# Attention before a soft mixture of experts: order of the first loads, place of the sums of values, and GpSimd keeping the statistics

## The chip, the cores and the metric

One Trainium2 chip, of which the kernel uses 1 core. The metric is the device time of one execution in microseconds (us). Names used: PE is TensorE, ACT is ScalarE, DVE is VectorE, POOL is GpSimd, SP is the engine that issues the transfers.

## What is computed

The input x has 8 batches of 512 tokens with 256 features. Only the attention half matters here:

```
xn   = layernorm(x)                                   # per token, no scale or shift
q,k,v = xn @ w_qkv.T, split into 16 heads of 16
dots = q @ k.T                                        # per head, no softmax
attn = dots / max(norm(dots over j), 1e-12) * g + b   # g, b: one number per head
out  = (attn @ v) @ w_out.T + b_out
x    = x + layernorm(out)
```

A second block follows, a soft mixture of 8 experts with 128 slots each (dispatch and combine weights by softmax, two weight layers with GELU, layernorm, residual). The change does not touch it.

## The kernel before

**Method.** As the attention has no softmax, the 512 x 512 scores are never formed. With G = xn^T xn (256 x 256, the "Gram" product), k^T v = wk G wv^T, so per batch the kernel computes G, then G times the key weights (`gk`), then per pair of head groups the head products k^T k and k^T v (`heads`), masked to the diagonal blocks of the heads. The outputs are q times the masked k^T v, the squared norms are sums over q * (k^T k q) (`qGq`). The bias b of the attention multiplies the sum of the values over the tokens, `vb`, which comes from the sums of xn over the tokens (`xsum`, an extra column of the Gram product) times the value weights: `value_sums`. Queries do not come from xn: they use the raw x transposed in DRAM (`xT`), with weights whose column mean has been subtracted, as the missing division by the standard deviation cancels in the normalised scores.

**Precision.** TensorE multiplies float32r operands. Each float32 operand is split in a rounded high part (ACT writes it, `round_...`) and the rest (DVE subtracts, `rest_of_...`), and a product takes three passes: high x high, high x low, low x high. So ahead of each product stands the chain ACT rounding, DVE rest. From batch 3 on the Gram product takes two passes and is completed by its own transpose (`transpose_gram`, `add_transposed`).

**Order.** Each engine has one hand-written instruction stream, and semaphores tie them together. Attention is a software pipeline over batches: in step b, PE's `attention(b)` runs the front of batch b and the back of batch b - 1 in this order: `gram_of_x(b)` (L821), `gram_times_q(b-1)` (L894), `transpose_gram(b)` (L830), `outputs(b-1)` (L904), `norms(b-1)` (L914), `queries(b)` part 0 (L884), `gram_times_k(b)` (L843), `queries(b)` part 1 (L884), in batches 0, 1, 3, 5 and 7 `value_sums(b)` (L865), `transpose_o(b-1)` (L922), `head_products(b)` (L854), `projection(b-1)` (L931). Batches 3 to 6 are a hardware loop of two steps; "odd" in the code is the odd batch, which computes the sums of two batches at once in bank 0 of PSUM. Norms and Gram times keys share bank 3. Batch 0 has a front only.

ACT's `attention(b)` copies the Gram, takes squares and roots of the layer norms of batch b - 2 (L1407, L1414, L1427), keeps the sums of x (`keep_xsum`, L1350), rounds the Gram (L1364), copies the queries (`keep_qT`, L1381), rounds `gk` (L1374) and the transposed outputs `oT` (L1395), and then xn and xT of the next batch (L1314, L1316, L1332). DVE's `attention(b)` adds the projection's bias (L2126), takes the statistics of batch b + 1 (L1990, L1995), `qGq` (L2082), the Gram's rest (L2046), clamps the norms (L2090), inverts and scales the outputs (L2097, L2101), normalises batch b + 1 (`norm_x`, L2008, four tiles), copies its mean and variance to `mv_x` and its floor to `norm_floor` (L2014, L1938), in odd batches `vb` (`keep_sums`, L2071), then the rest of `gk` (L2076), the rest of `oT` (L2112), the masked heads (`keep_heads`, L2061 and L2062), and the rest of the next xn and xT (L2030, L2034).

**Opening.** SP issues, in this order: x of batch 0 in two halves, the identity, query weights, key and value weights, xT of batch 0 (L555 to L560), and after x has landed the next loads. DVE's `norm_first` normalises batch 0 in halves and then copies its statistics. PE sums the query weights (L965), DVE centres them (L1932). Then, before batch 0's products, ACT rounds key and value weights (L1452), query weights (L1454) and xT (L1332), and DVE takes the rests in the same order (L1926, L2034), then the Gram's (L2049). PE's `queries` wait for both weight parts, `gram_times_k` for the first.

POOL has in the attention stage only the centring of the output weights and bias (L707, L710); later it works on the dispatch weights.

## Time and profile before

| | |
|---|---|
| median of 3 runs | 821.07 us (820.95 to 821.4) |
| the profiled execution | 820.74 us, its span 818.9 us |
| busy share of the span | PE 99%, weight loads 88%, DVE 85%, ACT 77%, POOL 21% |
| granted TensorE clock | full in all 40 slices of the span |
| attention stage | from the start to about 149 us, where the projection beside batch 7's front ends |

A page of the profile describes one execution. Busy shares are averages over stages; for the question what a reordering is worth, the chain of waits (what released each instruction, followed back from the end) and the timelines of the engines in the attention stage are the views to read. Matmuls overlap in their pipeline, so their listed durations are longer than the distance from one to the next.

### The profile page before, as it was taken

How to read it: one execution, taken by the hardware profiler on the slowest of the kernel's cores; microseconds unless marked ns; L12 is line 12 of the kernel's file. 1: busy time of each engine (PE TensorE's matmuls, PEld its weight loads, DVE VectorE, ACT ScalarE, POOL GpSimd, SP SyncE). 2: the span in 40 equal slices, each digit the busy share in tenths (PEclk: the TensorE clock that was granted, in tenths of full speed). 3: DMA queues.
4: the chain of work that ended last, by engine and by line, in shares of the span. 5: the costliest groups of instructions: out<-in, count | busy, mean ns of one | idle time of the engine just before them, and what ended most of it. 6: DMA issues, size and time to landing. Idle time of an engine off the chain costs nothing.

```text
span 818.9 us, 16585 instructions
## 1 busy us (share of the span) xinstructions
PE 807.9 (99%) x5186; PEld 718.8 (88%) x5186; DVE 699.0 (85%) x1373; ACT 630.4 (77%) x1269; POOL 168.4 (21%) x211
## 2 busy tenths in 40 slices
PE   8999999999999999999999999999999999999997
PEld 7888888888888888887998999999999999999997
DVE  8798988799999989998958888888888889487776
ACT  5676766667786886789668888988888888777775
POOL 0100000033223333552420414141413122000000
PEclk9999999999999999999999999999999999999999
DMA  8322230102323253225102011020202020376893
GB/s 295 132 78 78 78 126 28 52 26 91 104 91 126 81 205 103 78 80 172 58 1 83 22 46 58 21 81 4 99 0 102 0 102 0 102 245 199 280 296 112
DMA packets 55011, 80.63 MB, mean 98 GB/s; under 512 B 3248, under 2 KB 33840, under 8 KB 54832
## 3 DMA queue, kind: packets, MB, share of 16 engines
q1 hardware_dynamic: 54960, 80.00, 29.0%
q8 instruction: 25, 0.41, 0.2%
q14 instruction: 26, 0.21, 0.1%
HBM read 54.83 MB, written 25.17 MB: 98 GB/s over the span
## 4 chain that ended last, share of the span: by engine, by line
PE 85%; DVE 5%; ACT 2%; issue 2%; POOL 0%; ACTq 0%; DVEq 0%; POOLq 0%
PE bank L1138 22%; PE bank L1182 17%; PE bank L1247 11%; PE bank L1025 9%; PE bank L1000 8%; PE bank L1130 3%; PE bank L1009 2%; PE bank L931 2%; PE bank L884 2%; PE bank L904 1%; PE bank L914 1%; PE bank L894 1%; PE bank L821 1%; PE bank L843 1%; PE bank L990 1%
## 5 line engine op out<-in xcount | busy, mean ns | idle before, releaser
L1138 PEld LDWEIGHTS bank<-w_r,act_r 128*128 128x128 f32 x1536 | 199.2, 190 | 11.3 <-issue 1.0
L1138 PE MATMUL bank<-w_r,act_r 128*128 128x256 f32 x1536 | 202.7, 282 | 0.0
L1025 PE MATMUL bank<-disp_r,y_r 128*128 128x512 f32 x384 | 103.4, 406 | 0.6 <-DVE disp_r L2297 0.4
L1000 PE MATMUL bank<-yT_r,snT 128*128 128x512 f32 x384 | 100.3, 397 | 0.0
L2509 DVE TENSOR_TENSOR act_r<-act,act_r 128x512 fp32r<-128x512 f32 x112 | 82.4, 742 | 18.8 <-ACT act_r L1708 18.7
L1247 PE MATMUL bank<-eo_r,comb_r 128*128 128x258 f32 x768 | 92.1, 282 | 0.0
L1247 PEld LDWEIGHTS bank<-eo_r,comb_r 128*128 128x128 f32 x768 | 92.0, 189 | 0.0
L1182 PE MATMUL bank<-snT,w_op 128*128 128x512 f32 x336 | 87.7, 395 | 0.2 <-DVE act L2503 0.2
L1000 PEld LDWEIGHTS bank<-yT_r,snT 128*128 128x128 f32 x384 | 71.6, 188 | 16.4 <-issue 0.5
L1025 PEld LDWEIGHTS bank<-disp_r,y_r 128*128 128x128 f32 x384 | 67.7, 189 | 13.3 <-DVE disp_r L2297 1.0
L1708 ACT ACTIVATE act_r<-act 128x512 fp32r<-128x512 f32 x112 | 70.9, 633 | 10.1
L1547 ACT ACTIVATE disp<-neg_lt,neg_max 128x512 f32<-128x512 f32 x56 | 40.4, 722 | 37.1 <-DVE neg_lt L2263 37.0
L1182 PEld LDWEIGHTS bank<-snT,w_op 128*128 128x128 f32 x336 | 59.5, 189 | 10.3 <-DVE act L2503 0.6
L1182 PE MATMUL bank<-w_first,w_op 128*128 128x512 f32 x252 | 67.5, 394 | 0.0
L716 POOL TENSOR_SCALAR disp<-disp,rz_disp 128x512 f32<-128x512 f32 x56 | 40.9, 729 | 124.0 <-DVE rz_disp L2292 124.0
L767 POOL TENSOR_TENSOR w_sum<-stage 128x128 f32<-128x128 f32 x28 | 16.6, 594 | 203.5 <-DMA stage<-in_w 120.5
L2503 DVE TENSOR_TENSOR act<-bank,act 128x512 f32<-128x512 f32 x56 | 38.5, 688 | 14.4 <-PE bank L1182 12.7
L1182 PEld LDWEIGHTS bank<-w_first,w_op 128*128 128x128 f32 x252 | 43.7, 190 | 6.2 <-DVE act L2503 0.2
L1701 ACT ACTIVATE act<-act,b_sb 128x512 f32<-128x512 f32 x56 | 40.1, 716 | 9.9 <-DVE act L2503 8.8
L2297 DVE TENSOR_TENSOR disp_r<-bank,disp_r 128x512 fp32r<-128x512 f32 x64 | 43.6, 682 | 4.8 <-ACT disp_r L1559 4.4
L1574 ACT ACTIVATE comb<-comb,zero_col 128x512 f32<-128x512 f32 x64 | 45.3, 714 | 1.6 <-DVE comb L2286 1.5
L1559 ACT ACTIVATE disp_r<-bank 128x512 fp32r<-128x512 f32 x64 | 37.4, 585 | 10.5 <-PE bank L1009 10.5
(235 smaller groups left out, 1637.1 us busy)
## 6 DMA issues: line engine op xcount, KB each, us to landing
combine_scratch<-comb SPq DMA_DIRECT2D x64, 256.0 KB, 2.0
stage<-in_w SPq DMA_DIRECT2D x16, 1024.0 KB, 5.5
stage<-combine_scratch SPq DMA_DIRECT2D x4, 2048.0 KB, 9.1
snT<-combine_scratch SPq DMA_DIRECT2D x4, 2048.0 KB, 9.4
slots_eo<-in_x_t SPq DMA_DIRECT2D x8, 512.0 KB, 6.1
x_scratch<-stage SPq DMA_DIRECT2D x8, 512.0 KB, 3.2
x<-x_scratch SPq DMA_DIRECT2D x8, 512.0 KB, 4.4
x_d<-x_scratch SPq DMA_DIRECT2D x8, 512.0 KB, 9.7
```

What stands on the lines that cost most here:

```text
L716: nc.gpsimd.tensor_scalar(dispatch(b, m), dispatch(b, m), dispatch_cols(b, m)[2], 1.0, ALU.mult, ALU.mult).then_inc(disp_normed, 1)
L1000: last = pe.matmul(bank[m % 2][:, :], snT[:, i, k, m * S:(m + 1) * S], yT_r[:, j, k, :], start=(n == 0), stop=(n == len(steps) - 1))
L1025: last = pe.matmul(bank[4 + k][:, :], y_r[:, i, t, k * P:(k + 1) * P], disp_r[h][:, j, t, :], start=(n == 0), stop=(n == len(fill_steps) - 1))
L1138: done = pe.matmul(bank[BH + 2 * f + c // 2][:, (c % 2) * D:(c % 2 + 1) * D], act_r[:, tile, a, c * S:(c + 1) * S], w2_r[:, w, j, :], star ...
L1182: done = pe.matmul(target[:, :], w1_op[:, g % 2, a, LEFT_AT[n], :], slot_operand(n)[:, c, :], start=(n in (0, 3) and s == 0), stop=(s == 2 ...
L1247: done = pe.matmul(bank[4 * u + t][:, 0:DZ], comb_r[:, m % RING, i, t * P:(t + 1) * P], eo_r[u][:, j, m, :], start=(m == 0 and n == 0), st ...
L1547: act_fn(dispatch(b, m), neg_logits(b, m), ACT.Exp, bias=least, scale=-1.0, accum_out=total).then_inc(disp_exp, 1)
L1574: act_fn(comb[:, m % RING, :], comb[:, m % RING, :], ACT.Exp, bias=zero_col[:], scale=-1.0)\
L1701: act_fn(kept_tile(g, tile), source, ACT.Gelu, bias=b1_sb[:, ds(e * KH + j, 1)]).then_inc(h_act, 1)
L1708: act_fn(act_r[:, tile, 0, :], kept_tile(g, tile), ACT.Copy).then_inc(h_hi, 1)
L2297: v.tensor_tensor(disp_r[h][:, 1, :, cols], bank[2 + m % 2][:, :].rearrange("p (t s) -> p t s", t=NT), disp_r[h][:, 0, :, cols].bitcast(F3 ...
L2509: v.tensor_tensor(act_r[:, tile, 1, :], kept_tile(g, tile), act_r[:, tile, 0, :].bitcast(F32), ALU.subtract).then_inc(h_split, 1)
```

## The change

- SP's first loads: xT of batch 0 moves ahead of the key and value weights, the identity moves to the end of the group.
- ACT and DVE in batch 0: xT first, then query weights, then key and value weights. PE's `queries` wait for the query weights' split only, `gram_times_k` for both. The semaphores for summed and centred query weights become one.
- The sums of values of odd batches move from behind the second query product to between `outputs` and `norms`, now into bank 3 behind the norms' columns (batch 0 still in bank 0, at the old place). PE waits for a new semaphore of ACT, `xsum_kept`, and `gram_times_k` waits for `vb_kept`, since it overwrites that bank. `keep_sums` moves to right behind `clamp_norm` on DVE. The wait of the even batches' queries for `vb_kept` goes.
- The copy to `mv_x` and the floor go from DVE to POOL (`keep_stats`), for batches 0 and 1 ahead of POOL's weight centring, for the others behind it; DVE's next `bn_aggr` waits for them.
- DVE normalises the next batch in two halves of two tiles in all batches, with the rest of `gk` (and in batch 1 that of the output weights) between them.
- `keep_heads` masks both head groups of k^T k in one instruction instead of two.

The diff, with the renamed semaphores' declarations left out:

```diff
@@ -411,6 +411,9 @@
+        def sums_at(b):
+            return (bank[0], 0) if is_batch(b, 0) else (bank[3], NT * KD * HPT)
         def heads_bank(b):
@@ -553,11 +556,11 @@
                 sp.dma_start(xin[:, rows, :], x_v[:, rows, :]).then_inc(first_loaded[c], 16)
-            sp.dma_start(ident[:], identity).then_inc(ident_loaded, 16)
             wqkv_v = wqkv_t.rearrange("(k p) o -> p k o", p=P)
             sp.dma_start(wqkvT[:, :, 0:D], wqkv_v[:, :, 0:D]).then_inc(wq_loaded, 16)
+            sp.dma_start(xT[:, 0], xt_v[:, 0:KD, :]).then_inc(xT_loaded[0], 16)
             sp.dma_start(wqkvT[:, :, D:3 * D], wqkv_v[:, :, D:3 * D]).then_inc(wkv_loaded, 16)
-            sp.dma_start(xT[:, 0], xt_v[:, 0:KD, :]).then_inc(xT_loaded[0], 16)
+            sp.dma_start(ident[:], identity).then_inc(ident_loaded, 16)
             for c in range(2):
@@ -702,12 +705,26 @@
         def _(pool):
+            def keep_stats(b):
+                pool.wait_ge(x_aggr, b + 1)
+                if is_batch(b, 0):
+                    pool.wait_ge(half_aggr, 1)
+                alone(pool)
+                nc.gpsimd.tensor_copy(mv_x[:, ds(b * NT, NT), :], mv[:])
+                nc.gpsimd.tensor_scalar(norm_floor[:, ds(b * NT, NT)], mv[:, :, 1], LN_EPS, NORM_EPS * NORM_EPS,
+                                        ALU.add, ALU.mult).then_inc(x_mean_kept, 1)
+            keep_stats(0)
+            keep_stats(1)
             for k in range(KD):
...
             nc.gpsimd.tensor_scalar(bout_bc[:], bout_bc[:], b_mean[:], None, ALU.subtract).then_inc(bout_centred, 1)
+            for b in range(2, B):
+                keep_stats(b)
@@ -831,12 +848,14 @@
-            def gram_times_k(b):
+            def gram_times_k(b, odd, it):
                 pe.wait_ge(gram_split, b + 1)
-                pe.wait_ge(wqkv_split, 1)
+                pe.wait_ge(wqkv_split, 2)
                 if not is_batch(b, 0):
                     pe.wait_ge(norm_clamped, b)
+                    if odd:
+                        pe.wait_ge(vb_kept, sums_through(b, True, it))
                 steps = [(k, i, j) for k in range(KD) for i, j in PASSES]
@@ -859,21 +878,23 @@
                 pair = slice(b, b + 1) if is_batch(b, 0) or is_batch(b, 1) else slice(0, 2)
-                pe.wait_ge(qT_ready, b * KD + 1)
+                where, at = sums_at(b)
+                if is_batch(b, 0):
+                    pe.wait_ge(qT_ready, 1)
+                else:
+                    pe.wait_ge(xsum_kept, b + 1)
                 for h in range(KD):
                     for k in range(KD):
-                        last = pe.matmul(bank[0][:, 2 * h + pair.start:2 * h + pair.stop],
+                        last = pe.matmul(where[:, at + 2 * h + pair.start:at + 2 * h + pair.stop],
                                          wqkvT[:, k, 2 * D + h * P:2 * D + (h + 1) * P], xsum[:, pair, k],
...
                 pe.wait_ge(xT_split, b + 1)
-                pe.wait_ge(wqkv_split, 2)
+                pe.wait_ge(wqkv_split, 1)
                 if is_batch(b, 1):
                     pe.wait_ge(vb_kept, 1)
-                elif not odd and not is_batch(b, 0):
-                    pe.wait_ge(vb_kept, sums_through(b - 1, True, it))
                 if symmetric(b):
@@ -943,11 +964,13 @@
                     outputs(b - 1, first_back)
+                    if odd:
+                        value_sums(b)
                     norms(b - 1)
                 queries(b, odd, it, [0])
-                gram_times_k(b)
+                gram_times_k(b, odd, it)
                 queries(b, odd, it, [1])
-                if odd or not back:
+                if not back:
                     value_sums(b)
@@ -963,7 +986,7 @@
                 last = pe.matmul(bank[7][:, 0:D], ones_f[:], wqkvT[:, k, 0:D], start=(k == 0), stop=(k == KD - 1))
-            last.then_inc(wq_summed, 1)
+            last.then_inc(wq_steps, 1)
             attention(0, False, back=False)
@@ -1347,11 +1370,12 @@
                     alone(sc)
-                    act_fn(xsum[:, u], gram[:, :, D:D + 1].rearrange("p k a -> p (k a)"), ACT.Copy)
+                    last = act_fn(xsum[:, u], gram[:, :, D:D + 1].rearrange("p k a -> p (k a)"), ACT.Copy)
                 else:
...
                     for m in range(KD):
-                        act_fn(xsum[:, u, m:m + 1], gram_bank(b, m)[:, D:D + 1], ACT.Copy)
+                        last = act_fn(xsum[:, u, m:m + 1], gram_bank(b, m)[:, D:D + 1], ACT.Copy)
+                last.then_inc(xsum_kept, 1)
@@ -1448,11 +1472,11 @@
                 if front and not back:
+                    round_xT(0, False)
+                    sc.wait_ge(wq_steps, 2)
+                    act_fn(wqkv_r[:, 0, :, 0:D], wqkvT[:, :, 0:D], ACT.Copy).then_inc(wqkv_hi, 1)
                     sc.wait_ge(wkv_loaded, 16)
                     act_fn(wqkv_r[:, 0, :, D:3 * D], wqkvT[:, :, D:3 * D], ACT.Copy).then_inc(wqkv_hi, 1)
-                    sc.wait_ge(wq_centred, 1)
-                    act_fn(wqkv_r[:, 0, :, 0:D], wqkvT[:, :, 0:D], ACT.Copy).then_inc(wqkv_hi, 1)
-                    round_xT(0, False)
                 if symmetric(b):
@@ -1922,21 +1946,16 @@
                 cols = slice(D, 3 * D) if part else slice(0, D)
-                dve.wait_ge(wqkv_hi, 2 - part)
+                dve.wait_ge(wqkv_hi, part + 1)
                 v.tensor_tensor(wqkv_r[:, 1, :, cols], wqkvT[:, :, cols], wqkv_r[:, 0, :, cols].bitcast(F32),
...
-                dve.wait_ge(wq_summed, 1)
+                dve.wait_ge(wq_steps, 1)
                 v.scalar_tensor_tensor(out=wqkvT[:, :, 0:D], in0=bank[7][:, 0:D].unsqueeze(1).to_broadcast([P, KD, D]),
                                        scalar=-1.0 / D, in1=wqkvT[:, :, 0:D], op0=ALU.mult, op1=ALU.add)\
-                    .then_inc(wq_centred, 1)
-            def keep_floor(b):
-                v.tensor_scalar(norm_floor[:, ds(b * NT, NT)], mv[:, :, 1], LN_EPS, NORM_EPS * NORM_EPS,
-                                ALU.add, ALU.mult).then_inc(x_mean_kept, 1)
+                    .then_inc(wq_steps, 1)
@@ -1973,8 +1992,6 @@
                 last.then_inc(xn_ready, 1)
-                v.tensor_copy(mv_x[:, 0:NT, :], mv[:])
-                keep_floor(0)
                 dve.wait_ge(half_hi, 1)
@@ -1990,6 +2007,7 @@
                 dve.wait_ge(x_stats, b + 1)
+                dve.wait_ge(x_mean_kept, b)
                 alone(dve)
@@ -2008,11 +2026,10 @@
                 if end < NT:
-                    last.then_inc(half_normed, 1)
+                    if is_batch(b, 1):
+                        last.then_inc(half_normed, 1)
                 else:
                     last.then_inc(xn_ready, 1)
-                    v.tensor_copy(mv_x[:, ds(b * NT, NT), :], mv[:])
-                    keep_floor(b)
@@ -2057,8 +2074,9 @@
                     dve.wait_ge(o_in_psum, b)
+                v.tensor_tensor(heads[:, :, 0, :], heads_psum[:, :].rearrange("p (h d) -> p h d", h=KD)[:, :, 0:P],
+                                mask[:].unsqueeze(1).to_broadcast([P, KD, P]), ALU.mult)
                 for h in range(KD):
-                    v.tensor_tensor(heads[:, h, 0, :], heads_psum[:, h * D:h * D + P], mask[:], ALU.mult)
                     last = v.scalar_tensor_tensor(out=heads[:, h, 1, :], in0=heads_psum[:, h * D + P:(h + 1) * D],
@@ -2067,8 +2085,11 @@
                 n = pair.stop - pair.start
+                where, at = sums_at(b)
                 dve.wait_ge(sums_in_psum, sums_through(b, True, it))
-                v.tensor_tensor(vb[:, pair, :], bank[0][:, 0:2 * KD].rearrange("p (h a) -> p a h", a=2)[:, pair, :],
+                if not is_batch(b, 0):
+                    dve.wait_ge(norm_in_psum, b)
+                v.tensor_tensor(vb[:, pair, :], where[:, at:at + 2 * KD].rearrange("p (h a) -> p a h", a=2)[:, pair, :],
                                 b_col[:].unsqueeze(1).to_broadcast([P, n, KD]), ALU.mult).then_inc(vb_kept, 1)
@@ -2153,9 +2174,9 @@
                 if front and not back:
+                    rest_of_xT(0, False)
+                    rest_of_wqkv(0)
                     rest_of_wqkv(1)
-                    rest_of_wqkv(0)
-                    rest_of_xT(0, False)
                     rest_of_gram(0)
@@ -2173,22 +2194,23 @@
                     clamp_norm(b - 1)
+                if odd:
+                    keep_sums(b, it)
+                if back:
                     scale_o(b - 1)
...
                     invert_x_std(b + 1)
-                    norm_x(b + 1, 0, NT if back else NT // 2)
+                    norm_x(b + 1, 0, NT // 2)
                 if before_y:
                     make_y(0, False)
-                if odd:
-                    keep_sums(b, it)
                 if first_back:
...
                     rest_of_gk(b)
-                if front and not back:
-                    norm_x(1, NT // 2, NT)
+                if following:
+                    norm_x(b + 1, NT // 2, NT)
                 if back:
```

## Rows read from the trace of the kernel before

**Rows 1.** The page, part 4: shares of the chain of waits by engine.

```profile
PE 85%; DVE 5%; ACT 2%; issue 2%; POOL 0%; ACTq 0%; DVEq 0%; POOLq 0%
```

**Rows 2.** Timeline of PE, opening: start us, duration us, engine, line, operation [idle before <-releaser].

```profile
7.99 3.13 PE L821 MATMUL bank<-xn_r 128*128 128x258 f32 x24 [0.19 <-DVE xn_r L1979]
12.31 1.65 PE L884 MATMUL bank<-xT_r,wqkv_r 128*128 128x512 f32 x6 [1.19 <-DVE xT_r L2034]
13.80 1.60 PE L843 MATMUL bank<-wqkv_r,gram_r 128*128 128x256 f32 x12
...
17.43 1.67 PE L854 MATMUL bank<-wqkv_r,gk_r 128*128 128x256 f32 x12
19.63 3.11 PE L821 MATMUL bank<-xn_r 128*128 128x258 f32 x24 [0.53 <-DVE xn_r L2024]
```

**Rows 3.** Chain of waits, batch 4 (start us, us, what), and one PE row of the timeline.

```profile
80.71 1.79 PE bank L904 x16
...
87.11 1.40 PE bank L884 x6
...
88.53 0.45 ACT qT L1381
...
90.57 0.75 DVE oT_r L2112
...
91.36 2.99 PE bank L931 x24
...
89.55 1.70 PE L854 MATMUL bank<-wqkv_r,gk_r 128*128 128x256 f32 x12 [0.18 <-DVE gk_r L2076]
```

**Rows 4.** Chain of waits, batch 3, and one ACT row of the timeline.

```profile
61.69 1.79 PE bank L904 x16
...
68.53 1.38 PE bank L884 x6
...
63.30 0.19 ACT L1350 ACTIVATE xsum<-gram 128x2 f32<-128x2 f32 x1
```

**Rows 5.** Timeline of ACT, then DVE, opening; columns as in rows 2.

```profile
8.14 1.06 ACT L1452 ACTIVATE wqkv_r<-stage 128x1024 fp32r<-128x1024 f32 x1 [0.28 <-DMA stage<-in_wqkv_t]
9.21 0.63 ACT L1454 ACTIVATE wqkv_r<-stage 128x512 fp32r<-128x512 f32 x1
9.93 1.06 ACT L1332 ACTIVATE xT_r<-slots_eo 128x1024 fp32r<-128x1024 f32 x1
...
9.23 1.83 DVE L1926 TENSOR_TENSOR wqkv_r<-stage,wqkv_r 128x1024 fp32r<-128x1024 f32 x2
11.03 1.23 DVE L2034 TENSOR_TENSOR xT_r<-slots_eo,xT_r 128x1024 fp32r<-128x1024 f32 x1
12.17 0.75 DVE L2049 TENSOR_TENSOR gram_r<-bank,gram_r 128x256 fp32r<-128x256 f32 x2
```

**Rows 6.** DMA issues at 2.73 and 3.24: queue, count, KB, us to landing.

```profile
stage<-in_wqkv_t SPq DMA_DIRECT2D x1, 512.0 KB, 5.4
...
slots_eo<-in_x_t SPq DMA_DIRECT2D x1, 512.0 KB, 6.7
```

**Rows 7.** Timeline of DVE, end of batch 0; columns as in rows 2.

```profile
16.07 0.69 DVE L2076 TENSOR_TENSOR gk_r<-bank,gk_r 128x512 fp32r<-128x512 f32 x1
...
17.97 0.69 DVE L2020 TENSOR_TENSOR xn_r<-xn,xn_r 128x512 fp32r<-128x512 f32 x1 [0.41 <-ACT xn_r L1322]
```

**Rows 8.** Timeline of POOL, then DVE, where both subtract or take minima.

```profile
166.79 1.31 POOL L723 TENSOR_TENSOR y_r<-y,y_r 128x512 fp32r<-128x512 f32 x1
...
167.20 1.45 DVE L2277 TENSOR_TENSOR run_min<-run_min,slots_eo 128x512 f32<-128x512 f32 x1
...
172.58 0.74 DVE L2277 TENSOR_TENSOR run_min<-run_min,slots_eo 128x512 f32<-128x512 f32 x1
```

**Rows 9.** Chain of waits, batch 5, and one ACT row of the timeline.

```profile
100.23 1.69 PE bank L914 x16
...
99.69 0.19 ACT L1350 ACTIVATE xsum<-gram 128x2 f32<-128x2 f32 x1
```

More of the change, by code:

```diff
@@ L239, in attention_then_soft_moe @@
         snT_ready = sem("snT_ready")
-        wq_summed = sem("wq_summed")
-        wq_centred = sem("wq_centred")
+        wq_steps = sem("wq_steps")
         wqkv_hi = sem("wqkv_hi")
@@ L266, in attention_then_soft_moe @@
         xT_split = sem("xT_split")
+        xsum_kept = sem("xsum_kept")
         gram_in_psum = sem("gram_in_psum")
```

## The prediction

> **What bounds the kernel now.** I read the page first. The chain of waits lies on TensorE for 85% of the span, DVE has 5%, ACT 2% [rows 1]. What a change of order can win is therefore the time in which TensorE stands still, so I then read the timeline of TensorE through the attention stage, which the change alone touches. Batch 0's Gram product starts at 7.99 us and takes 3.13, to 11.12; the query product starts at 12.31, released by the low part of x transposed; Gram times keys follows at 13.80, the head products at 17.43, the next Gram at 19.63 after a wait of 0.53 [rows 2]. So the opening has one hole of 1.19 us. Next I read, per batch, the time before the head products (a wait for `gk_r`, row 89.55 of [rows 3], 0.18 on PE) and the chain of waits through an even batch. That chain does not go through `gk_r` at all. It goes from the end of the second query product (87.11 + 1.40 = 88.51) over ACT's copy of qT at 88.53, the rounding of oT, DVE's rest of oT at 90.57, to the projection at 91.36: 2.85 us [rows 3]. Last, I compared the same stretch, outputs to second query product, in two batches: 61.69 to 68.53 = 6.84 us in batch 3, 80.71 to 87.11 = 6.40 in batch 4 [rows 3, 4]. Batch 3 loses 0.44 to small waits, for qGq and the Gram's low part.
>
> **The sum's scale.** The profiled execution took 820.74 us, its span 818.9; the median of the runs is 821.07, 0.33 above. I work out a difference and take it from the median.
>
> **Loads and order of the query path (batch 0).** Before, ACT rounded the key and value weights from 8.14 (1.06 us), the query weights from 9.21 (0.63), x transposed from 9.93 (1.06); DVE did its parts as one unbroken run from 9.23 to 12.92: weights 1.83, x transposed 1.23 from 11.03, Gram 0.75 from 12.17 [rows 5]. The transfer of x transposed was issued at 3.24 and landed 6.7 later, at 9.94; the larger weights, one place ahead, landed 5.4 after 2.73, at 8.13 [rows 6]. The swap puts x transposed in that place, and the identity (now last; first used at 19.6) no longer stands before it. With two issues of some 0.5 each (2.73 to 3.24) fewer ahead it is issued at about 2.25; bounds for the landing: 2.25 + 5.4 = 7.65, and 2.25 + 6.7 = 8.95. I take 8.0, as the weights landed at 8.13 from that place. Then ACT: x transposed 8.05 to 9.1, query weights 9.2 to 9.85, key and value weights to 10.9. DVE, still from 9.23, takes x transposed to 10.4, query weights to 11.0, the rest to 12.2, the Gram to 12.92 as before. The queries need only the first two, so they start at 11.15, not 12.31, and end at 12.6; Gram times keys then waits for DVE's 12.92 and starts at 12.97, not 13.80: 0.83 us gained. The same block takes 3.63 to the head products (13.80 to 17.43 [rows 2]), so PE would be there at 16.6; `gk_r`'s rest was done at 16.07 + 0.69 = 16.76 [rows 7] and comes at 16.65. Head products at 16.7: **0.73 gained**. To reach the next Gram with it, DVE's low part of xn must come sooner: DVE stood idle 0.41 before it [rows 7], waiting for ACT, which waited for PE; 0.1 comes from above, and the two small operations that leave DVE are a part of the 0.80 it worked before (16.76 to 17.56). Together 0.6 to 0.7; I book **0.7**; bounds 0 (landing at 8.95: Gram times keys at 13.8 again) and 0.85.
>
> **Statistics copied by GpSimd.** Two small DVE operations per batch go to POOL, hidden on either engine in batches 2 to 7, where PE sets the pace. DVE's next aggregation waits for POOL's copy, one batch later, which is the cover. If POOL were late, `mv`'s next aggregate, and behind it DVE's whole queue, would be. In the opening DVE is on the path. What POOL costs DVE is bounded by one place: DVE's 128x512 minimum took 1.45 us at 167.20 while POOL's subtraction ran (1.31 from 166.79), and 0.74 at 172.58 without it [rows 8]. So each POOL operation may hold DVE by 0 to 0.71. These are of 4 to 8 columns, not 512, so I take 0.05 each for the two of batch 0: **-0.1**.
> The Trainium skill (SBUF — State Buffer, "SBUF: two separate sides") says that the shared port pair is locked for a whole instruction and the second comer fully blocks; the minimum's row agrees. By that rule, normalising on DVE and the copies on POOL exclude each other, and what is left to ask is how long POOL holds on; that is the rival below.
>
> **Sums of values beside the norms (odd batches).** Same eight matmuls, moved from behind the second query product to ahead of the norms. Order on PE after the move: sums, norms, queries, Gram times keys, queries, transposes. PE arrives at the transposes at the same moment, and from the end of the queries the 2.85 us over ACT and DVE hold as in an even batch: **0**. What is later by their length (8 times the 0.125 us worked out below, 1.0): norms, clamp, square root, scaled outputs; Gram times keys, too. The cover is that between the norms and the transposes, which need the scaled outputs, three products still stand, each nearly the 1.49 us from 12.31 to 13.80 [rows 2], an estimated 4.4 us. New is PE's wait for the kept sums of x, and behind it queue the norms and all later work. ACT writes them in batch 3 at 63.30 to 63.49 [rows 4], PE is done with the outputs at 61.69 + 1.79 = 63.48: even. In batch 5 ACT is ready at 99.88, PE at 100.23 [rows 9]: 0.35 to spare. In batch 3 the sums fill the time in which PE waited for qGq and for the Gram's low part, so the 0.44 go to between 0 (if PE waits for ACT instead) and 0.44; DVE, which feeds ACT there, comes a little sooner, its two small operations being gone. I book **0.4**.
>
> **Low part of Gram times keys amid the normalisation.** DVE does it after two tiles instead of four and the copies: some 0.7 us sooner, as two tiles and the two small operations make up most of the 0.80 above. In the even batch of [rows 3] the head products then start without their wait; but the projection behind them waits for oT, whose chain starts at the query product and is untouched. The wait moves behind them: **0**. The same in batches 1, 2 and 6. Merging the masks of two heads saves DVE one instruction, beside the projection: 0. The wait of the even queries for `vb_kept` was not in the chain: 0.
>
> Sum: 0.7 - 0.1 + 0.4 = 1.0 us; later stages depend on PE's progress and shift with it. 821.07 - 1.0 = **820.1**.
>
> **Rivals.** (a) The waits before the head products are won after all, because oT comes sooner than I think: DVE reaches it with less behind it. Of the 2.85 us PE works some 2.5 (8 transposes and 12 products at the 2.99 / 24 = 0.125 of the projection [rows 3]; an estimate), so 0.35 a batch is to be had, in four batches 1.4: **818.7**. For: the waits are real. Against: DVE itself waits for ACT in that chain. (b) The opening wins nothing, because x transposed lands near 8.95: **820.8**. For: other transfers run beside it, and the landing from the new place cannot be read from before. Against: the weights in that place landed at 8.13. (c) Slower: GpSimd blocks DVE in the opening. Place: POOL's copies start with the finished statistics of batches 0 and 1, just when DVE begins to normalise them, on the path both times. Price: four operations at up to 0.71 = 2.84; 821.07 - 1.1 + 2.84 = **822.8**. It decides from 1.1 / 4 = 0.28 us of hold each. For: the lengthened minimum. Against: the size. (d) PE's wait for the sums of x takes the batch 3 gain: **820.5**; the time stays within 0.2%.
>
> **How the numbers follow.** 0.2% is 1.64 us, about what a measurement of this kernel tells from no change. Forecast 0.45, (a) 0.2, (b) 0.17, (c) 0.08, (d) 0.1. Faster needs under 819.43: (a) and a tail of the forecast, 0.25 together. Slower needs over 822.71: half of (c) and what I overlooked, 0.07. Same 0.68. The range runs from a little under (a), 818.5, to the middle of (c), 821.6 (four holds of about 0.4).
>
> **What would show it.** Right: queries of batch 0 at about 11.1, Gram times keys near 13.0, next Gram near 18.9; sums between outputs and norms with no more than 0.2 of wait; in even batches no wait before the head products and a longer one before the projection, 2.85 after the queries as before; DVE's first normalisation no longer than before. Wrong: the projection coming less than 2.7 us after the queries (a); ACT's rounding of x transposed starting after 8.5 (b); DVE operations of the opening lengthened beside POOL's (c); idle on PE ahead of the sums (d).

## The result, and the profile after

The changed kernel takes 823.54 us (median of 15 runs, 821.92 to 825.58); the kernel before, beside it, 820.95 (15 runs). The ratio is 1.0024, its 95% interval 1.0013 to 1.0035: slower by 0.24%, where 820.1, a small gain, and a range of 818.5 to 821.6 were forecast. The profiled execution took 823.76 us.

The page of the changed kernel, parts 1 and 4: TensorE is as busy as before, and its share of the chain of waits is 87%, not 85 [rows 1]. It works longer (810.8 us for 807.9), it doesn't wait longer.

```profile
span 822.0 us, 16575 instructions
...
PE 810.8 (99%) x5186; PEld 721.9 (88%) x5186; DVE 698.6 (85%) x1349; ACT 630.0 (77%) x1269; POOL 169.9 (21%) x227
...
PE 87%; DVE 6%; ACT 3%; issue 2%; DMA 1%; POOL 0%; SPq 0%; ACTq 0%; DVEq 0%; POOLq 0%
```

The timeline of PE in the opening (columns as in rows 2) answers to [rows 2]. The hole of 1.19 us before the first query product (L905 here, L884 before) has shrunk to 0.42; Gram times keys starts at 13.06 instead of 13.80, the head products at 16.81 instead of 17.43, the next Gram at 19.15 instead of 19.63.

```profile
11.36 1.63 PE L905 MATMUL bank<-xT_r,wqkv_r 128*128 128x512 f32 x6 [0.42 <-DVE wqkv_r L1950]
13.06 1.69 PE L862 MATMUL bank<-wqkv_r,gram_r 128*128 128x256 f32 x12
...
16.81 1.70 PE L873 MATMUL bank<-wqkv_r,gk_r 128*128 128x256 f32 x12
19.15 3.11 PE L838 MATMUL bank<-xn_r 128*128 128x258 f32 x24 [0.65 <-DVE xn_r L2041]
```

The timelines of ACT, DVE and POOL and a DMA issue, answering in part to [rows 5] and [rows 6]: of ACT the rounding of x transposed, of DVE the first normalisation, of POOL the two copies of batch 0, and the transfer of x transposed (issued at 2.26, landed 6.0 later).

```profile
8.29 1.06 ACT L1355 ACTIVATE xT_r<-slots_eo 128x1024 fp32r<-128x1024 f32 x1 [0.54 <-DMA slots_eo<-in_x_t]
...
5.49 0.75 DVE L1985 TENSOR_SCALAR xn<-slots_eo,mv,rstd 128x256 f32<-128x256 f32 x2
...
5.58 0.19 POOL L713 COPY mv_x<-mv 128x8 f32<-128x8 f32 x1 [5.14 <-DVE mv L1978]
5.85 0.19 POOL L714 TENSOR_SCALAR norm_floor<-mv 128x4 f32<-128x4 f32 x1
...
slots_eo<-in_x_t SPq DMA_DIRECT2D x1, 512.0 KB, 6.0
```

In batch 4 the chain of waits (start us, us, what) and two rows of PE's timeline answer to [rows 3]. The head products (L873) start at once behind the transposes, and the projection (L952) now has the wait. From the end of the second query product, 86.32 + 1.40 = 87.72, to the projection are 2.86 us, before 2.85.

```profile
86.32 1.40 PE bank L905 x6
...
87.75 0.45 ACT qT L1405
...
88.91 0.69 ACT oT_r L1419
...
89.78 0.75 DVE oT_r L2133
...
88.34 1.68 PE L873 MATMUL bank<-wqkv_r,gk_r 128*128 128x256 f32 x12
90.58 3.09 PE L952 MATMUL bank<-wout_r,oT_r 128*128 128x256 f32 x24 [0.56 <-DVE oT_r L2133]
```

In batch 3 the chain, and ACT's row for the kept sums of x, answer to [rows 4]. From the outputs to the second query product are 68.58 - 61.24 = 7.34 us, of which the sums are 0.84; the other 6.50 were 6.84. ACT has kept the sums at 62.56 + 0.19 = 62.75, before PE is done with the outputs at 63.03.

```profile
61.24 1.79 PE bank L925 x16
63.02 0.84 PE bank L888 x8
...
68.58 1.39 PE bank L905 x6
...
62.56 0.19 ACT L1373 ACTIVATE xsum<-gram 128x2 f32<-128x2 f32 x1
```

So far nearly all is as forecast: the projection of batch 4 starts at 90.58 instead of 91.36, 0.78 us sooner. Then the time is lost in two places. The timeline of PE, batches 4, 5 and 7: in batch 5 the first query product and Gram times keys last 2.39 and 2.41 us, in batch 4 the same instructions 1.64 and 1.60; in batch 7 they last 2.77 and 2.03. Ahead of the long ones stand the sums (L888, 2 columns each) and the norms (L935, 8 columns each).

```profile
83.25 1.64 PE L905 MATMUL bank<-xT_r,wqkv_r 128*128 128x512 f32 x6
84.72 1.60 PE L862 MATMUL bank<-wqkv_r,gram_r 128*128 128x256 f32 x12
...
99.37 0.95 PE L888 MATMUL bank<-xsum,stage 128*128 128x2 f32 x8
100.18 1.93 PE L935 MATMUL bank<-head_sel,qGq 128*128 128x8 f32 x16
101.97 2.39 PE L905 MATMUL bank<-xT_r,wqkv_r 128*128 128x512 f32 x6
104.16 2.41 PE L862 MATMUL bank<-wqkv_r,gram_r 128*128 128x256 f32 x12
...
138.20 1.93 PE L935 MATMUL bank<-head_sel,qGq 128*128 128x8 f32 x16
139.99 2.77 PE L905 MATMUL bank<-xT_r,wqkv_r 128*128 128x512 f32 x6
142.56 2.03 PE L862 MATMUL bank<-wqkv_r,gram_r 128*128 128x256 f32 x12
```

The view by stretches gives the reason (columns: stretch, its length, busy time of the engines with their instructions, the clock granted to TensorE, DMA share, GB/s). The granted clock stands at 1.00 up to the end of the norms (102.11 and 140.13 us) and falls within 0.5 us behind it to 0.50, from 2.4 to 1.2 GHz; over 102 to 106 us and over 140 to 144 us it averages 0.57.

```profile
core 0: us, PE busy (x) PEld busy (x) DVE busy (x) ACT busy (x) POOL busy (x), PEclk, DMA share, GB/s
99.00:102.00 3.00, 3.00 (x30) 3.00 (x29) 2.60 (x7) 2.21 (x8) 0.00 (x0) 1.00 0.00 0
102.00:106.00 4.00, 4.00 (x17) 3.52 (x17) 3.00 (x8) 1.92 (x6) 0.00 (x0) 0.57 0.91 270
138.00:140.00 2.00, 2.00 (x21) 2.00 (x20) 1.73 (x4) 1.20 (x4) 0.00 (x0) 1.00 0.00 0
140.00:144.00 4.00, 4.00 (x17) 3.42 (x17) 3.35 (x9) 1.92 (x6) 0.00 (x0) 0.57 0.38 131
```

A stretch of 4 us at 0.57 loses 4 x 0.43 = 1.72 us; from the projection of batch 4 to that of batch 5 are 110.76 - 90.58 = 20.18 us, before 109.86 - 91.36 = 18.50, so 1.68 more. Two falls are 3.44. The span is 822.0 against 818.9, longer by 3.1: less 3.44 it would be 818.6. PE is busy 3.00 of 3.00 us before the fall of batch 5 and 2.00 of 2.00 before that of batch 7; its record shows no idle time when the clock falls. The query products that run in the slow stretches are the same 512-column ones as in batch 4, where the clock stays at 1.00.

Every execution shows its mean granted clock: 0.994 to 0.998 in the 15 of the changed kernel, the fastest (821.92) at 0.997, the slowest (825.58) at 0.994. The number of such falls in an execution varies, and with it the time. The 15 executions stand in three groups: five at 821.92 to 822.20 (clock 0.997 and 0.998), seven at 823.23 to 824.32 (0.995 and 0.996), three at 825.13 to 825.58 (0.994). The steps are some 1.7 us, one fall each. One step below the first group, at an estimated 820.3 (their mean of 822.06 less 1.72), an execution without a fall would lie; none of the 15 does.

### The profile page after: what moved, and what is told of

The parts are those of the page before. It is cut to its first block, busy times and chain, and to the rows that moved or that the text cites. A ratio compares the mean times of both kernels' runs of the same rounds, so it can differ in the third digit from the quotient of the medians.

```text
span 822.0 us, 16575 instructions
## 1 busy us (share of the span) xinstructions
PE 810.8 (99%) x5186; PEld 721.9 (88%) x5186; DVE 698.6 (85%) x1349; ACT 630.0 (77%) x1269; POOL 169.9 (21%) x227
## 4 chain that ended last, share of the span: by engine, by line
PE 87%; DVE 6%; ACT 3%; issue 2%; DMA 1%; POOL 0%; SPq 0%; ACTq 0%; DVEq 0%; POOLq 0%
PE bank L1161 22%; PE bank L1205 17%; PE bank L1270 11%; PE bank L1048 8%; PE bank L1023 8%; PE bank L1153 3%; PE bank L905 3%; PE bank L952 3%; PE bank L1032 2%; PE bank L838 2%; PE bank L925 2%; PE bank L935 2%; PE bank L915 2%; PE bank L862 1%; DVE oT_r L2133 1%
## 5 line engine op out<-in xcount | busy, mean ns | idle before, releaser
L2285 DVE TENSOR_SCALAR_CACHE_REDUCE neg_lt<-bank,se_scale 128x512 f32<-128x512 f32 x56 | 41.6, 743 | 4.7 <-DVE comb L2308 2.5
```

What stands on the lines that cost most here:

```text
L2285: v.tensor_scalar(neg_logits(b, m), bank[m % 2][:, :], se_scale[:, m:m + 1], None, ALU.mult, ALU.min, accum_out=dispatch_cols(b, m)[0]).th ...
```

## The experiments

Theory A: the narrow matmuls of the sums directly ahead of the norms bring the falls. Theory B: another part of the change does (the new wait ahead of the projection, the shift of the stage). Theory C: the falls have nothing to do with the kernel, and both kernels vary alike. Each kernel was timed in several rounds beside the kernel before (820.91, 820.96 and 821.05 us in the three series).

### Sums back at their old place

```diff
                 if back:
                     outputs(b - 1, first_back)
-                    if odd:
-                        value_sums(b)
                     norms(b - 1)
...
                 queries(b, odd, it, [1])
-                if not back:
+                if odd or not back:
                     value_sums(b)
```

with bank 0 again, the waits that go with it, and `keep_sums` behind the second half of the normalisation.

> The changed kernel with the sums of values of odd batches at their old place (behind the second query product, bank 0); all else as changed. Theory A: the eight 2-column matmuls of the sums directly ahead of the sixteen 8-column ones of the norms are what TensorE's granted clock falls after (0.50 from about 102.6 to 106 us and again from about 140 to 143.3 us in the changed kernel's trace); apart, the clock stays at 1.00 throughout, and the time is 820.4 us (0.5 under the kernel before). Theory B: the fall comes from elsewhere in the change (the new wait of about 0.5 us ahead of the projection, or the shift of the whole stage by the shorter opening): the clock still falls, and the time stays near 823.5. Theory C: the fall is the chip's and has nothing to do with the kernel: both kernels vary alike.

Measured: 820.34 us (11 runs, 819.86 to 820.93), ratio 0.9988 [0.998, 0.9997]. The stretches of this kernel in which the changed one fell:

```profile
99.00:102.00 3.00, 3.00 (x27) 2.93 (x26) 2.80 (x8) 2.55 (x10) 0.00 (x0) 1.00 0.00 0
102.00:106.00 4.00, 4.00 (x26) 3.56 (x25) 3.51 (x10) 2.52 (x9) 0.00 (x0) 1.00 0.78 228
138.00:144.00 6.00, 6.00 (x42) 5.49 (x42) 4.55 (x11) 3.46 (x11) 0.00 (x0) 1.00 0.32 99
```

Theory A holds and B falls: the wait ahead of the projection is still there (0.5 to 0.8 us in batches 1 to 6), the opening is the changed one, and the clock stays. The rest of the change is worth 0.12%. Theory C as it was put falls too: the clock was 0.999 or 1.00 in all 11 executions here and in none of the 15 of the changed kernel. A part of it is true, though. The clock of the kernel before falls as well, only seldom: 9 of its 62 executions beside these experiments had 0.997 or 0.998, at 821.86 to 823.88 us; none of them was profiled, so where it falls there isn't known. The move makes frequent what was rare.

Batch 3 of this kernel bears on the prediction. From the outputs to the second query product are 67.88 - 61.29 = 6.59 us; before they were 6.84, in the changed kernel 6.50 without the sums.

```profile
61.29 1.95 PE L922 MATMUL bank<-heads,qT 128*128 128x128 f32 x16
...
67.88 1.56 PE L902 MATMUL bank<-xT_r,wqkv_r 128*128 128x512 f32 x6
```

### The kernel before, with only the sums moved

```diff
                     outputs(b - 1, first_back)
+                    if odd:
+                        value_sums(b)
                     norms(b - 1)
...
-                if odd or not back:
+                if not back:
                     value_sums(b)
```

with bank 3, ACT's semaphore for the kept sums of x, the wait for `vb_kept` ahead of Gram times keys, and `keep_sums` behind `clamp_norm` on DVE.

> The kernel before with only the sums of values of odd batches moved ahead of the norms, into bank 3, with the waits that go with it; old load order, old order on DVE, statistics on DVE. Theory A: the clock falls in one to four odd batches, each fall at about 1.7 us; the wait before Gram times keys in batch 3 goes (0.4): 822.2 to 825, the middle 823.7. Theory B: without the shorter opening and the new wait the clock holds, 820.5 to 821.

Measured: 826.81 us (6 runs, 823.23 to 827.51), ratio 1.0056 [1.0036, 1.0075], mean clock 0.990 to 0.997. Three falls in the profiled execution, in batches 1, 3 and 7:

```profile
31.00:35.00 4.00, 4.00 (x19) 3.68 (x18) 3.90 (x14) 1.68 (x3) 0.00 (x0) 0.57 0.21 83
...
68.00:73.00 5.00, 5.00 (x25) 4.42 (x26) 4.35 (x12) 2.63 (x10) 0.00 (x0) 0.66 0.63 181
...
143.00:148.00 5.00, 5.00 (x23) 4.46 (x24) 3.43 (x9) 2.04 (x7) 0.00 (x0) 0.66 0.31 107
```

The move alone does it, without any other part of the change. The time is above what was expected (822.2 to 825), and in the profiled execution not all of that is the falls'. Its span of 824.9 us is 6.0 over the kernel before; three falls make 5.1. Another 1.2 us are lost in the opening: batch 0's Gram product lasts 4.28 us (3.13 before), and the next one starts at 20.81 instead of 19.63. TensorE does 6 matmuls there in a microsecond in which it did 10 before, and yet the view gives the granted clock as 1.00 in both (first row before, second this kernel). No run shows why.

```profile
9.00:10.00 1.00, 1.00 (x10) 1.00 (x10) 0.95 (x2) 0.90 (x3) 0.00 (x0) 1.00 1.06 383
9.00:10.00 1.00, 1.00 (x6) 1.00 (x6) 0.49 (x1) 0.64 (x1) 0.00 (x0) 1.00 0.98 317
```

In the changed kernel it was batches 5 and 7 that fell: which odd batch falls isn't fixed by the program.

### Two and six wide matmuls between sums and norms

```diff
                     if odd:
                         value_sums(b)
+                        pe.wait_ge(xT_split, b + 1)
+                        if symmetric(b):
+                            pe.wait_ge(gram_kept, b - THIRD + 1)
+                        else:
+                            pe.wait_ge(vb_kept, 1)
+                            pe.wait_ge(gram_hi, b + 1)
+                        for _ in range(2):
+                            pe.matmul(bank[0][:, :], wqkv_r[:, 0, 0, 0:P], xT_r[:, 0, 0, :], start=True, stop=True)
                     norms(b - 1)
```

The second kernel has `range(6)`.

> The changed kernel with two more 512-column matmuls between the sums and the norms of each odd batch; their results go to bank 0 and are overwritten by the queries, so nothing computed changes. They are work of 2 x 0.24 us in four batches, 1.9 us. Theory A: they keep the clock at 1.00 and the kernel is no slower than the changed one although it does more: 822.3. Theory B or C: nothing changes in the clock, and the 1.9 us come on top: 825.4.

Measured with two: 824.27 us (11 runs, 822.67 to 827.48). Neither number was met; in the trace the two matmuls put the norms 0.55 us later, 2.2 us in the four batches, not 1.9. The falls remain, one in the profiled execution, in batch 1:

```profile
28.00:32.00 4.00, 4.00 (x17) 3.43 (x17) 2.65 (x10) 0.71 (x2) 0.81 (x3) 0.57 0.75 286
```

This run alone is inconclusive: its mean clock over the runs (0.9963) can't be told from the changed kernel's (0.9959). So the same with six:

> As the kernel with two 512-column matmuls between sums and norms, which still fell in clock (mean 0.996), now with six: 4 x 6 x 0.21 = 5.2 us of own work. With the first query product of that length between them the clock had held. If the distance between the sums and the norms is what counts, the clock is 0.999 or 1.00 and the time 820.4 + 5.2 = 825.6; if the order as such (sums first, norms behind) brings the falls, the clock stays near 0.996 and the time is 828.5.

Measured with six: 825.90 us (5 runs, 825.83 to 826.47), clock 0.999 to 1.00 in every one, where 825.6 was expected. Two of the stretches at and behind the norms:

```profile
26.00:30.00 4.00, 4.00 (x29) 3.70 (x30) 0.15 (x2) 0.42 (x3) 1.26 (x3) 1.00 0.95 351
...
70.00:74.00 4.00, 4.00 (x31) 3.69 (x30) 3.33 (x8) 2.86 (x7) 0.00 (x0) 1.00 0.71 255
```

The order is the changed kernel's, sums first and norms behind, with more work; the clock holds and the runs agree within 0.1%. The six put the norms 1.47 us later by the trace (batch 1: sums 25.59, norms 27.87, without them 0.81 apart), 5.9 us in four batches; the 5.2 of the expectation was too low.

### Sums between the first query product and Gram times keys

```diff
                     outputs(b - 1, first_back)
-                    if odd:
-                        value_sums(b)
                     norms(b - 1)
                 queries(b, odd, it, [0])
+                if odd and not is_batch(b, 1):
+                    value_sums(b)
                 gram_times_k(b, odd, it)
+                if odd and not is_batch(b, 1):
+                    pe.wait_ge(vb_kept, sums_through(b, True, it))
                 queries(b, odd, it, [1])
```

with bank 1 for batches 3, 5 and 7, and `keep_sums` behind `scale_o`; batch 1 has its sums at the old place.

> The changed kernel with the sums of values of batches 3, 5 and 7 still early, but between the first query product and Gram times keys (bank 1), so that each is between full products; batch 1 has them at the old place. Theory A: the neighbours count, not how early the sums stand or that PE waits for ACT's kept sums: clock 1.00, 820.4 us, as with the sums at their old place. Rival: an early place as such brings the fall: near 823.

Measured: 820.63 us (12 runs, 820.0 to 821.51), ratio 0.999 [0.9981, 0.9998], clock 0.999 or 1.00 in all. Early sums are no harm as such, nor is PE's wait for the kept sums of x; with the first query product between the norms and the sums the clock holds.

### The sums' matmuls twice

```diff
-                for h in range(KD):
+                for h in [h for _ in range(1 if is_batch(b, 0) else 2) for h in range(KD)]:
                     for k in range(KD):
```

> The changed kernel with the sums' matmuls issued twice in odd batches (the second round overwrites the first with the same values), so that the stretch of narrow matmuls with the norms lasts 3.4 us instead of 2.6. Own work: 4 x 0.8 = 3.2 us. If the length of the narrow stretch is the cause, the clock falls in all four odd batches of nearly every execution (granted clock 0.991 and under) and the time is 829 to 831. If the falls come with another cause, as often as in the changed kernel: 823.5 + 3.2 = 826.7 at a clock of 0.996.

Measured: 832.45 us (4 runs, 829.91 to 834.25), clock 0.988 to 0.991. The stretches with falls in the profiled execution, the last one twice as long:

```profile
68.00:72.00 4.00, 4.00 (x18) 3.69 (x17) 2.66 (x6) 2.10 (x7) 0.00 (x0) 0.57 0.97 284
...
106.00:110.00 4.00, 4.00 (x16) 3.42 (x16) 3.00 (x8) 1.92 (x6) 0.00 (x0) 0.58 0.91 268
143.00:151.00 8.00, 8.00 (x36) 7.37 (x36) 3.82 (x10) 2.08 (x8) 0.00 (x0) 0.57 0.24 73
```

The dose counts: 0.9 us more of narrow work in four places (by the trace; 0.8 was expected) cost 8.9 us over the changed kernel, of which 3.6 are the work. The expected 829 to 831 was too low, although in the profiled execution only batches 3, 5 and 7 fall, not all four: a fall can last longer. Over 143 to 151 us the clock averages 0.57 for 8 us.

### The opening alone, and the rest without it

The first is the kernel before with the loads in the new order, ACT `round_xT(0)`, query weights, key and value weights, DVE likewise, and PE's two waits for `wqkv_split` exchanged. The second is the changed kernel with the sums back and the old opening.

```diff
             sp.dma_start(wqkvT[:, :, 0:D], wqkv_v[:, :, 0:D]).then_inc(wq_loaded, 16)
+            sp.dma_start(xT[:, 0], xt_v[:, 0:KD, :]).then_inc(xT_loaded[0], 16)
             sp.dma_start(wqkvT[:, :, D:3 * D], wqkv_v[:, :, D:3 * D]).then_inc(wkv_loaded, 16)
-            sp.dma_start(xT[:, 0], xt_v[:, 0:KD, :]).then_inc(xT_loaded[0], 16)
```

> The kernel before with only the opening changed: x transposed ahead of the key and value weights, identity last, and ACT, DVE and PE of batch 0 in that order. If the opening is worth what the trace of the changed kernel shows at batch 1's Gram product (19.15 us against 19.63, less 0.15 that came from the small copies taken off DVE), it gives 0.3 to 0.5: 820.5 us. If later waits eat it, 820.9.

> The changed kernel with the sums at their old place and the old opening; what is left of the change is the statistics on GpSimd, the split normalisation and the merged mask. By the trace of the changed kernel these give batch 3's small waits back (0.3) and 0.1 in the opening: 820.6 us. If the split normalisation only moves waits, as the prediction held, 820.9.

Measured: the opening alone 820.32 us (12 runs, 819.98 to 823.16; ratio 0.9998 [0.9988, 1.0008]); the rest alone 820.74 (11 runs; 1.0001 [0.9992, 1.001]). The medians are within 0.2 us of those expected, 0.64 and 0.22 under the kernel before, but the intervals hold 1, so neither gain is clear of noise, as 2 of the 12 and 1 of the 11 executions had the clock at 0.997 and took some 823. PE's timeline of the first shows Gram times keys at 13.16 and the next Gram at 19.22, 0.64 and 0.41 sooner than in [rows 2]:

```profile
13.16 1.69 PE L843 MATMUL bank<-wqkv_r,gram_r 128*128 128x256 f32 x12
...
19.22 2.99 PE L821 MATMUL bank<-xn_r 128*128 128x258 f32 x23 [0.65 <-DVE xn_r L2024]
```

### A version that beats both

The wait before the projection hangs on the end of the second query product. So the transposes of the outputs can go ahead of that product, which then lies beside ACT's and DVE's work on oT.

```diff
                 gram_times_k(b, odd, it)
+                if odd:
+                    value_sums(b)
+                if back:
+                    transpose_o(b - 1)
                 queries(b, odd, it, [1])
                 if not back:
                     value_sums(b)
-                if back:
-                    transpose_o(b - 1)
+                head_products(b)
                 if before_y:
                     transpose_y(0, 0, first=True, to=0)
-                head_products(b)
```

with `round_oT` ahead of `keep_qT(b, 1)` on ACT, `keep_sums` ahead of `rest_of_gk` on DVE, and the sums in bank 0, no longer beside the norms.

> The changed kernel with the sums of values between Gram times keys and the transposes of the outputs (bank 0), and with the transposes ahead of the second query product, so that this product lies beside the rounding of oT; ACT rounds oT before it copies the second qT, DVE keeps the sums before the low part of Gram times keys, and batch 7 transposes y behind the head products. The traces so far show the wait ahead of the projection (0.5 to 0.8 us on PE in batches 1 to 6) as what the split normalisation turned the earlier wait into, with a chain that runs from the end of the second query product. If that chain is what holds the projection, most of it is hidden now: 0.35 a batch in six batches, 2.1 less than with the sums at their old place, 818.3 us; where the scaled outputs come late for the transposes (DVE, even batches, 0.3) less, 819.3. If the projection waits for DVE's other work instead, 820.3 as with the sums at their old place. The narrow sums and the norms are kept apart by two full products, so the clock should hold at 0.999 or 1.00.

Measured: 817.50 us (6 runs, 817.2 to 819.78), ratio 0.9953 [0.9936, 0.9969]: 3.5 us under the kernel before, and 0.8 under the 818.3 expected. PE's timeline of batch 4, from the first query product (L902) over Gram times keys, transposes, second query product and head products to the projection (L949):

```profile
84.54 1.63 PE L902 MATMUL bank<-xT_r,wqkv_r 128*128 128x512 f32 x6
...
87.80 1.09 PE L940 MATMUL bank<-ident,o_tok 128*128 128x128 f32 x8 [0.20 <-DVE o_tok L2117]
88.65 1.63 PE L902 MATMUL bank<-xT_r,wqkv_r 128*128 128x512 f32 x6
90.12 1.60 PE L871 MATMUL bank<-wqkv_r,gk_r 128*128 128x256 f32 x12
91.55 2.99 PE L949 MATMUL bank<-wout_r,oT_r 128*128 128x256 f32 x24
```

From the first query product to the projection are 91.55 - 84.54 = 7.01 us; in the changed kernel they are 90.58 - 83.25 = 7.33. The wait has gone from the projection to the transposes (0.20, for DVE's scaled outputs) and shrunk. Odd batches gain more: from `gram_times_q` in batch 5 to the one in batch 6 are 114.06 - 96.31 = 17.75 us here and 114.41 - 95.82 = 18.59 in the kernel with the sums back, in the even batch 4 17.42 and 17.83. The clock did not hold at 0.999 as expected: 2 of the 6 executions have 0.997. The profiled one is the slowest of the six, 819.78 us; it has the long first Gram product of above (4.35 us) and a fall behind the norms of batch 3, without sums beside them:

```profile
65.00:69.00 4.00, 4.00 (x17) 3.42 (x17) 3.55 (x9) 2.93 (x10) 0.00 (x0) 0.57 0.45 134
```

## Why the prediction was wrong

The step that failed is "**Sums of values beside the norms**", booked at 0 with the words "Same eight matmuls, moved" and "PE arrives at the transposes at the same moment". The instructions and the waits were counted, but TensorE's clock was taken as given: none of the rivals has it. The move put 0.8 us of 1- or 2-column matmuls directly ahead of 1.8 us of 8-column ones, and behind them the granted clock fell from 2.4 to 1.2 GHz in some of the odd batches, at 1.72 us each. Two falls in the profiled execution make 3.44, and 820.34 (without the move) against 823.54 (with it) is 3.2. That the new neighbourhood brings the falls is shown by undoing the move, by doing it alone, by six wide matmuls in between, and by doubling the sums. The kernel before held 0.999 or 1.00 in 53 of 62 executions, the changed one in none of 15.

What stays open is which property of these matmuls counts. The sums and the norms are narrow, and they are also plain float32 matmuls, of which the trace has two records for each in the code, where the query products are float32r in three passes (not all products of this kernel are float32r, as the description of its precision has it). No run changed the width alone. Nor does a run show why one execution falls in batch 5 and another in batch 1.

The Trainium skill (TensorE: Matmul & The Clock Gate, "HAM oscillation — how this bites in real kernels") ties a fall of the clock to gaps in which PE is idle. Here the engine's record is busy throughout the stretch before the fall (3.00 of 3.00 us and 2.00 of 2.00). By that section the move would have been free here; the rows disagree, and they decide.

The other steps, in the prediction's order:

- *Opening, 0.7 booked, bounds 0 and 0.85.* At the next Gram 0.48 were gained, with the two small copies gone; alone, the opening gave 0.41 there and 0.64 in the median. Queries were expected at 11.15, came at 11.36, as x transposed landed at 2.26 + 6.0 = 8.26, not 8.0. Gram times keys: 12.97 forecast, 13.06 measured. Rival (b), no gain, is out.
- *POOL's copies, 0.1 lost booked.* Each took 0.19 us; DVE's first normalisation lasts 0.75 us (0.73 before), and POOL's rows, 5.58 to 6.04, lie inside it (5.49 to 6.24); if one engine held up the other there, it was by 0.02 us on DVE, though spans on POOL are rough. Rival (c), the only one on the slower side, is out: the time came out slower by another cause, so that it lies near this rival's 822.8 is chance.
- *Batch 3's small waits, 0.4 booked.* 0.34 measured. But the kernel with the sums back has 0.25 of it, so only 0.09 comes from sums that fill a wait; the rest comes with DVE being sooner, which the prediction named second. Rival (d), PE waiting for the kept sums, is out: ACT was ready 0.28 before PE.
- *Low part of Gram times keys amid the normalisation, 0 booked.* Right in its mechanism: no wait at the head products, and 2.86 us to the projection for 2.85. Rival (a), 818.7, is out; what it hoped for came with the transposes moved, at 817.5.
- *The sum* without the clock was 1.0. The estimated 820.3 without falls is 0.65 under the kernel before; the kernel with the sums back, to which only 0.7 - 0.1 = 0.6 of the sum applies, gained 0.57. In the traces the changed kernel was ahead by 0.78 at batch 4's projection and, less two falls, by 149.14 - 3.44 = 145.70 against 146.40, or 0.70, at batch 7's. From there to the end it was 0.36 longer (822.0 - 149.14 = 672.86 against 818.9 - 146.40 = 672.50). That tail runs from 672.5 (sums back) to 673.0 us (two wide matmuls) in kernels that all have the same code there, so the 0.36 isn't shown to be a cost of the change.

## What to carry to other kernels

Before matmuls with few columns are moved, look at which others they will stand next to. TensorE's clock, not its instruction count, can be what the new order costs (here two falls, 3.44 us, with not one instruction more on TensorE); read the granted clock stretch by stretch, and the durations of the same wide product in different iterations. And a wait that an edit removes is worth something only if the chain of waits goes through it; here it went past it, and what paid was to reorder along that chain.

## What the hardware did unexpectedly

- The granted clock fell to half while PE was recorded as busy without a gap, behind 2.6 us of matmuls with 1 to 8 columns, and stayed down for about 3.4 us (4 us at 0.57), also through 512-column products. In the kernel with doubled sums it stayed down twice as long once. In the trace of the kernel with the transposes first it fell behind the norms alone (1.8 us).
- The changed kernel fell one to three times an execution (each fall takes 1.72 / 820 = 0.0021 off the mean clock of 0.998 to 0.994), which made its times spread by 0.45% (821.92 to 825.58), where kernels that held the clock agree within 0.2%. The kernel with the move alone fell in other odd batches.
- Six more wide matmuls per odd batch, 5.9 us of work, cost 2.4 us over the changed kernel, as they end the falls: the 3.5 us between are two of them.
- In two profiled executions (the move alone, and the transposes first) the first Gram product took 4.28 and 4.35 us instead of 3.13, at a granted clock given as 1.00. So a clock row of 1.00 in the opening doesn't show that TensorE ran at full rate there.
